# Quad sums at odd pairs, and the next chunk's steps one pair earlier, in a two-layer token-mixing kernel

## The reference

```python
x = x + L0_conv(ln_c(x), kernel_base)        # FFT, one complex 64x64 matrix for each of 32x32 kept modes, inverse FFT
t = to_tokens(x)
t = t + L0_ffn(ln_t(t), ...)                 # router, top 2 of 8 experts, weighted sum of their outputs
x = from_tokens(t, x)
x = x + L1_conv(ln_c(x), kernels)            # depthwise 29x29 convolution, zero padded
t = to_tokens(x)
t = t + L1_ffn(ln_t(t), ...)                 # a second mixture of experts
x = from_tokens(t, x)
```

## Time and profile before

| what | us |
|---|---|
| median of 3 runs | 986.98 |
| lowest and highest | 986.14, 988.03 |
| the profiled execution | 987.52 |
| its span | 985.70 |
| experts of layer 0, first pair to last sum copy | 209 to 473 |
| convolution on TensorE | 484.43 to 711 |
| experts of layer 1 | 711 to the end |

### The profile page before, as it was taken

The page is one execution under the profiler, slowest core; times in us unless marked ns, Lnnn a source line. Parts: engine busy times, 40 slices in busy tenths (PEclk is TensorE's granted clock), DMA queues, the critical chain, the costliest instruction groups (busy, mean ns, idle before and its releaser), DMA issues.

```text
span 985.7 us, 24665 instructions
## 1 busy us (share of the span) xinstructions
PE 879.0 (89%) x9610; PEld 724.8 (74%) x9610; DVE 780.4 (79%) x1461; ACT 508.0 (52%) x1051; POOL 561.6 (57%) x495
## 2 busy tenths in 40 slices
PE   6987899768799999899499999999848899999998
PEld 6987888745566676665499999999825666667665
DVE  5768576887799999999967776774687999897884
ACT  3467454579466766510244444444267666666511
POOL 3670000417788888789554433440116888889888
PEclk9997599979799999999799999999957999999999
DMA  9997000020799999601587778878200101101101
GB/s 377 335 324 240 25 1 1 2 51 2 302 366 375 387 375 374 270 1 39 213 271 269 262 268 272 268 261 272 71 1 1 44 23 44 44 23 44 44 26 61
DMA packets 48292, 163.35 MB, mean 166 GB/s; under 512 B 9296, under 2 KB 9808, under 8 KB 46032
## 3 DMA queue, kind: packets, MB, share of 16 engines
q1 hardware_dynamic: 48208, 162.20, 45.6%
HBM read 93.70 MB, written 68.49 MB: 165 GB/s over the span
## 4 chain that ended last, share of the span: by engine, by line
PE 58%; DVE 22%; POOL 6%; issue 5%; ACT 5%; DMA 3%; SPq 1%; POOLq 0%; DVEq 0%; ACTq 0%
PE pair L1695 23%; DVE R L905 7%; PE pair L1622 6%; PE pair L1608 5%; PE pair L1609 5%; PE pair L1571 4%; PE pair L1619 4%; DMA X<-x_rows 3%; PE pair L1494 3%; POOL R L568 3%; ACT pair L1251 2%; DVE R L658 2%; DVE R L845 2%; PE pair L1586 2%; DVE work L658 2%
## 5 line engine op out<-in xcount | busy, mean ns | idle before, releaser
L905 DVE TENSOR_TENSOR R<-pair,R 128x896 f32<-128x896 f32 x256 | 275.5, 1084 | 50.2 <-PE pair L1609 49.4
L568 POOL TENSOR_TENSOR R<-R 128x768 f32<-128x768 f32 x128 | 231.9, 1812 | 93.6 <-DVE R L905 79.2
L1695 PE MATMUL pair<-R 128*128 (+4 forms) x2880 | 226.4, 242 | 11.7 <-DVE R L983 11.7
L1695 PEld LDWEIGHTS pair<-R 128*128 128x128 f16 x2880 | 223.8, 98 | 14.4 <-issue 12.0
L1251 ACT ACTIVATE pair<-X,work 128x64 f32<-128x64 f32 x480 | 166.6, 394 | 123.3 <-DVE R L845 120.8
L1608 PE MATMUL pair<-work,R 128*128 128x448 f16 x512 | 186.4, 364 | 23.9 <-DVE R L905 23.6
L1609 PE MATMUL pair<-work,R 128*128 128x448 f16 x512 | 185.5, 362 | 0.0
L578 POOL TENSOR_TENSOR R<-R 128x512 f32<-128x512 f32 x128 | 164.7, 1287 | 10.0
L1369 ACT COPY R<-R 128x1152 f32<-128x1152 f32 x64 | 82.3, 1286 | 122.5 <-PE pair L1695 122.5
L998 DVE COPY R<-R 128x1152 f32<-128x1152 f32 x64 | 89.5, 1398 | 67.1 <-PE pair L1695 66.3
L1622 PE MATMUL pair<-R,ident_sb 128*128 128x256 f32 x496 | 129.5, 384 | 0.0
(11 more groups left out here) (137 smaller groups left out, 1344.6 us busy)
## 6 DMA issues: line engine op xcount, KB each, us to landing
taps_halves<-R SPq DMA_DIRECT2D x128, 458.5 KB, 4.4
R<-taps_halves SPq DMA_DIRECT2D x64, 917.0 KB, 4.7
X<-x_tok SPq DMA_DIRECT2D x4, 2048.0 KB, 17.4
out<-X SPq DMA_DIRECT2D x15, 512.0 KB, 2.6
R<-spec_pairs SPq DMA_DIRECT2D x16, 272.0 KB, 4.8
X<-x_rows SPq DMA_DIRECT2D x4, 1024.0 KB, 10.8
R<-x_chan SPq DMA_DIRECT2D x4, 1024.0 KB, 13.8
X<-x_rows SPq DMA_DIRECT2D x2, 2048.0 KB, 27.6
```

What stands on the lines that cost most here:

```text
L568: pool.tensor_tensor(pr[:, :, 192:384], pr[:, :, 0:192], pr[:, :, 192:384], ALU.add).then_inc(half_ready, 1)
L905: dve.tensor_tensor(pr.rearrange("p t (e c) -> p t e c", c=C), pair[p % 2][:, :].rearrange("p (t e c) -> p t e c", t=2, c=C)[:, :, 0:NE - ...
L1695: mm = pe.matmul(acc[:, y0:y1, x0:x1, :], blocks[i % 2][:, ks, 2 - y, 1 - x, :], src[:, y0 + y:y1 + y, x0 + x:x1 + x, :], start=(ks == 0 a ...
```

## The change

The quad sums move from even to odd pairs: quad g stands ahead of pair 2g+5 instead of 2g+6, on chunk 0 and on the others, and the extra sum behind the last chunk's loop becomes the one at its pair 15. The transposes move one pair up, as do routes 2 and 3, the sum copies on ScalarE, the exponential, and the gates' steps, whose fifteenth stays at pair 14. `normalise`, `low_parts`, the statistics, the seed and the Newton steps keep their pairs. The tap stores wait for 12 + 17p/20 weighed pairs instead of 12 + 2p/3. GpSimd waits for the low halves of VectorE's plane before plane 1, and no longer between its two operations. The scratch of the roots lies elsewhere.

```diff
--- before.py
+++ after.py
@@ -156,7 +156,7 @@
         o += 2048
         stat_all = R1[:, 14336:14336 + NT * 3].rearrange("p (t k) -> p t k", k=3)
         plane_shift, plane_root = work[:, 0:NT], work[:, NT:2 * NT]
-        plane_tmp = [R1[:, 5120 + NT * i:5120 + NT * (i + 1)] for i in range(5)]
+        plane_tmp = [R1[:, 8960 + NT * i:8960 + NT * (i + 1)] for i in range(5)]
         high = R1[:, 0:NT * C // 2].bitcast(F16).rearrange("p (c t) -> p c t", c=C)
         low = R1[:, NT * C // 2:NT * C].bitcast(F16).rearrange("p (c t) -> p c t", c=C)
 
@@ -262,7 +262,7 @@
         NOCT = NPAIR // 4
 
 
-        NORM_AT, LOW_AT, TURN_AT, ROUTE_AT = (4, 8, 12, 0), (6, 10, 14, 2), (9, 13, 1, 5), (0, 1, 3, 7)
+        NORM_AT, LOW_AT, TURN_AT, ROUTE_AT = (4, 8, 12, 0), (6, 10, 14, 2), (8, 12, 0, 4), (0, 1, 2, 6)
         FIRST_ROUTE = (2, 5, 7, 9)
         START_NORMS = {1: (1, 2), 3: (1, 3), 5: (2, 0), 8: (2, 1), 12: (2, 2)}
         START_LOWS = {1: (1, 1), 3: (1, 2), 5: (1, 3), 7: (2, 0), 10: (2, 1), 14: (2, 2)}
@@ -271,10 +271,10 @@
         START_PARTS = (2, 3, 4, 4, 5, 6, 7, 8)
         START_EXP = 13
         NORM_AHEAD, LOW_AHEAD, TURN_AHEAD = 3, 3, 2
-        COPY_AT, SUM_LAG, QUAD_LAG = 1, 2, 3
-        GATES_AT = {8: (0, 1), 9: (2, 3), 10: (4, 5), 11: (6, 7), 12: (8, 9), 13: (10, 11), 14: (12, 13, 14)}
+        COPY_AT, SUM_LAG, QUAD_FROM = 0, 2, 5
+        GATES_AT = {7: (0, 1), 8: (2, 3), 9: (4, 5), 10: (6, 7), 11: (8, 9), 12: (10, 11), 13: (12, 13), 14: (14,)}
         PARTS_AT = (0, 1, 1, 3, 3, 4, 5, 7)
-        EXP_AT, ROOT_AT = 12, 11
+        EXP_AT, ROOT_AT = 11, 11
         NEWTON_AT = 6
         POOLED = (2, 5, 8, 11)
 
@@ -421,7 +421,7 @@
             sp.wait_ge(taps_step, TAPS_STEPS)
             for p in range(P):
                 at = (WI - 1 - p // HI) * PITCH + HI - 1 - p % HI
-                sp.wait_ge(y_used, 12 + 2 * p // 3)
+                sp.wait_ge(y_used, 12 + 17 * p // 20)
                 sp.dma_start(taps_dram[:, :, p, :].rearrange("s c n -> (s c) n"),
                              taps_16[:, at:at + WINDOW]).then_inc(taps_out, 16)
             sp.wait_ge(taps_out, P * 16)
@@ -619,8 +619,6 @@
                 shift, root = (m.unsqueeze(1).to_broadcast([P, 4, NT]) for m in (plane_shift, plane_root))
                 pool.tensor_tensor(dst, src, shift, ALU.add).then_inc(plane_centred, 1)
                 pool.wait_ge(plane_centred, g)
-                if isinstance(g, int):
-                    pool.wait_ge(plane_normed, 1)
                 pool.tensor_tensor(dst, dst, root, ALU.mult).then_inc(plane_normed, 1)
 
             for layer in range(2):
@@ -646,6 +644,7 @@
                     expert_chunk(layer, k, k % 2, False)
                 if layer == 0:
                     pool.wait_ge(plane_step, PLANE_STEPS)
+                    pool.wait_ge(plane_low, 1)
                     normalise_plane(1, 1)
                     with pool.Fori(1, GROUPS // 2) as m:
                         normalise_plane(2 * m, 0)
@@ -1649,8 +1648,8 @@
 
             def start_chunk(layer):
                 for p in range(NPAIR):
-                    if p % 2 == 0 and p >= 2 * QUAD_LAG:
-                        sum_quad(layer, 0, 0, p // 2 - QUAD_LAG)
+                    if p % 2 == 1 and p >= QUAD_FROM:
+                        sum_quad(layer, 0, 0, (p - QUAD_FROM) // 2)
                     expert_pair(layer, 0, 0, p)
                     if p in START_TURNS:
                         k, j = START_TURNS[p]
@@ -1660,8 +1659,8 @@
 
             def expert_chunk(layer, k, q, following, normed):
                 for p in range(NPAIR):
-                    if p % 2 == 0:
-                        g = p // 2 - QUAD_LAG
+                    if p % 2 == 1:
+                        g = (p - QUAD_FROM) // 2
                         sum_quad(layer, k if g >= 0 else k - 1, q if g >= 0 else 1 - q, g % NQUAD)
                     expert_pair(layer, k, q, p)
                     if following and p in TURN_AT[TURN_AHEAD:]:
@@ -1732,7 +1731,6 @@
                 expert_chunk(layer, 5, 1, True, True)
                 expert_chunk(layer, 6, 0, True, False)
                 expert_chunk(layer, 7, 1, False, False)
-                sum_quad(layer, NCHUNK - 1, 1, NQUAD - 3)
                 sum_last(layer)
                 if layer == 0:
                     pe.wait_ge(y_used, NCHUNK * NPAIR)
```

## The result

The changed kernel took 996.55 us (median of 4, 996.27 to 997.01), the kernel before in the same session 986.93 (986.14 to 988.03): ratio 1.0097, 95% interval 1.0080 to 1.0115. The forecast was 991.5, at most 995.5: the sign was right, the size forecast was half of what was measured. The span of the profiled execution went from 985.70 to 995.22, +9.5 for a sum of +4.5.

What follows compares the result with a forecast made beforehand. TensorE was taken to set the time, but not alone: three engines nearly full, so order inside the chunk decides. 4.6 - 0.4 + 2.8 + 1.9 - 1.9 - 2.5 = +4.5 gave 992.0 profiled, 991.5 median; range 984.5 to 995.5.

Steps and rivals of the forecast that it cites:

- Quads, chunks 1 to 4: Chunks 1 to 4 of each layer: odd-pair quads lengthen each chunk by 0.57 us, eight times, +4.6 (0 to 8).
- The loop: From weigh 13 through GpSimd's Newton steps, quad 7 and weigh 7 to weigh 13: 30.59 us against 30.02 a chunk.
- the next longest loop: Weigh 7 to weigh 14, its low part, transpose at pair 0, TensorE to pair 7: 30.0 us without the GpSimd part.
- Chunks 5 to 7: Layer 1: chunk 5 -0.4, chunks 6 and 7 +2.8 by the two-quad loop of 3.46; layer 0: 0 and +1.9.
- Start chunks: Chunk 0 of both layers: quad 0 fits ahead of a transpose where TensorE waits; -1.9 in all, 0 to 3.2 a layer.
- The filled stop: TensorE's 3.35 us wait before a start-chunk transpose in layer 1, to be filled by quad 0; gain taken as 1.0.
- First plane: Before the convolution: GpSimd waits for VectorE's plane 0, so the 2.91 us multiply takes 0.4; -2.5 (0 to -2.6).
- Tap stores: The last store waits for weigh 119 instead of 96, with 11 us of cover; cost 0.
- clock stays up: Rival: the clock stays at its fast level in the start chunks, 1.5 us less, 990.0; chance 0.09.
- GpSimd in time: Rival at the quad sums: loop and Newton steps stay hidden, 4.6, 2.8 and 1.9 vanish, 982.2 us; chance 0.17.
- only the ends bind: Rival: the 4.6 of chunks 1 to 4 vanishes, 986.9 us; chance 0.18.
- no earlier convolution: Rival: the 2.91 us multiply is not GpSimd's doing, so the convolution starts no earlier, 994.0 us; chance 0.10.

Runs made afterwards that it cites:

- the tail on even pairs: The changed kernel with the quads of chunks 6 and 7 of both layers, and their sum copies, on even pairs again: 993.54 us, ratio 1.0066 to the kernel before.

## Why the prediction missed

1. *Quads, chunks 1 to 4*: right. The loop, the stop at quad 7 and 30.59 are as worked out (in the chunk of layer 1 shown, 9.19 + 1.64 + 7.07 + 0.96 + 11.74, where the forecast had 9.18 + 1.60 + 7.08 + 0.96 + 11.77), and so is the next longest loop of 30.0, which showed at 30.10 once the Newton steps were spread. One sentence of it was wrong: the moved gates and transposes "by themselves bring nothing". That held only beside odd quads; by themselves they bring 1.0. It left the sum alone, but it hid that the quads cost 1.56 a chunk, 0.49 by the Newton loop and 1.07 by their place, and that the others were the part to keep.
2. *Chunks 5 to 7*: layer 1's 2.8 for the last chunk was right (8 x (3.485 - 3.115) = 3.0; the tail on even pairs gave 3.0 back, both layers together). Chunk 5's -0.4 came out at -0.1, and layer 0's +1.9 at +1.0 (under 4).
3. *Start chunks*, -1.9: **the step that failed.** I had named the sum copy as the reason for a lower end of 0; it makes the lower end a loss, and the sum had no term for it. Quad 2 waits for the copy, and pair 9, its transpose and weigh 9 stand behind quad 2. Less the 0.57 forecast for each chunk 1, the start chunks' two stretches of the table lost 2.4 in one profile of this kernel and 0.9 in the other, for a forecast gain of 1.9. The filled stop itself was real: with the copies early, odd quads take about 1 off each start chunk (the table of the three orders). And I took the clock for a gain that might come or not. The new stop of 1.66 in layer 0 gave it a new place to fall, and a fall there cost 2.3. In layer 1 the start chunk came out no worse than with the old order (36.4), and 1.5 of what it and chunk 1 lost is a fall in chunk 1 that the old order has about as often (three profiles of four, three of five with the changed order); the profile before, on which the forecast stood, had been spared it. That part of the miss is the luck of one profile, not the change.
4. *First plane*: the 2.5 ahead was right, "what is gained ahead of it stays" was not: 0.9 came back, 0.2 of it in channel 0 (5.40 for 5.24, the clock) and the rest behind it, where the trace shows GpSimd's second plane beside VectorE's unpacking, 3.00 in place of 0.75. The kernel before has such slow copies too (2.87 at 489.67 in its trace), but far enough ahead of channel 4 that TensorE doesn't stop. Layer 0's end, before the convolution, came out 0.9 cheaper than forecast, so that the stretch hit by luck: two misses cancelled.
5. *Tap stores*: right; in the profile no engine waits for them.

The remaining 0.8 lies ahead of everything that was changed: from profile to profile the first weigh falls between 216.2 and 217.8. In the rivals, "clock stays up" had the right doubt; its gain did not show in the sum, since the clock fell elsewhere. "GpSimd in time" and "only the ends bind" were out by the period of 30.59, "no earlier convolution" by the wait of 9.16.

What stays open: how often the clock falls at each of these stops in executions without a profile. Their mean granted clock is on record: 0.944 to 0.946 in all eight executions of the changed kernel, 0.945 and 0.946 in the two profiled ones, so as a whole the others lost about as much as these; where they lost it is not known.

## What to carry to other kernels

When one step is moved in several engines' queues at once, try each move alone: here one of them cost 1.56 us a chunk and the others brought 1.0, and the sum hid both. Ask in which stretch each piece of work stands: a sum of 1.61 moved out of a stretch that VectorE fills into one where TensorE sets the pace cost 1.07 a chunk by its place alone. A step moved ahead of others must have its inputs early as well, above all a small copy at the end of a third engine's queue. Before a forecast is set against one profile, see whether a second profile of the same order agrees: here the clock alone moved a chunk by 1.5.

## What the runs showed of the hardware that was not expected

A stop of TensorE of 1.66 or 2.00 us leaves the granted clock at either level in the same code (1.00 or 0.50 behind the same wait, above), and 1.5 to 2.3 us hang on it. Ahead of chunk 1's first route in layer 1 it fell in 11 of 18 profiles, with the old order as with the new. The Trainium skill ("TensorE: Matmul & The Clock Gate", What's actually happening) has activity release the clock; the traces agree with that, and show that it is not the order of the work alone that decides when.

VectorE's copies beside a GpSimd add on SBUF took 3.00 in place of 0.75. The Trainium skill ("SBUF — State Buffer", Who interferes with whom) says that a VectorE instruction in a two-port mode, which copies can enter, and one of GpSimd contend for a shared pair of ports, and that the one that comes second blocks until the other's instruction ends; the trace agrees with that: the copy started at 496.42 and ended at 499.42, 0.63 after the add that ran from 495.89 to 498.79. With each plane behind the low halves of the one ahead and the cast later, VectorE's busy time in the whole kernel fell from 780 to 739 us (with the planes' waits alone it stayed at 780 to 782), and no time was gained by it: 982.90 us, where the same kernel without these two edits took 981.31. TensorE's 64 channels hid it.
